# A routed feed-forward behind a linear-attention pipeline: rows ranked and listed by expert sequence by sequence

## The chip, the cores and the metric

The kernel runs on one core of a Trainium2 chip. Time is device time of one launch in microseconds (us), the median of the runs. TensorE is PE in the profile, VectorE is DVE, ScalarE is ACT, GpSimd is POOL, and SyncE, which only issues DMAs here, is SP.

## What is computed

The input x is 8 sequences of 512 rows of 256 floats, 4096 rows in all. First a gated linear attention, then a feed-forward with 8 experts, of which each row uses the one whose centroid it is nearest to:

```python
x = x + attn(layernorm(x), wq, wk, wv, wo, wg1, wg2, norm_w)
z = layernorm(x).reshape(-1, 256)
aff = z @ centroids.T                       # 4096 x 8
assign = argmax(aff, axis=1)
order = argsort(assign)
xs, es = z[order], assign[order]
alpha = sigmoid(aff[order] at es)
for e in range(8):
    h = relu(layernorm(xs, ln_g[e], ln_b[e]) @ w1[e].T + b1[e])
    y = y + where(es == e, xs + h @ w2[e].T + b2[e], 0)
out_sorted = alpha * y + (1 - alpha) * xs
x = x + out_sorted[argsort(order)]
```

The kernel computes each row with its own expert alone. So it must know, for each tile of 128 rows, which expert the tile belongs to and which rows are in it. A tile holds rows of one expert; with 8 experts there are at most 32 + 7 = 39 tiles (`TILES`), and the last tile of an expert is filled up with rows whose result is not written.

## The kernel before

**The pipeline.** `pipeline` runs ten steps (i from 0 to 9) on every engine. In step i, sequence a = i is projected (q, k, v, gate, and GpSimd's tree of decays), sequence b = i - 1 runs the seven levels of the attention scores and its outputs, and sequence c = i - 2 is normed, projected by wo, added to x, normed again (`double_norm`), given its affinities to the centroids (`affinities`, L1215) and written out as rows (`rows_of`, `alphas`, and SP's store to `routed_rows`, L495). The order within a step is written out by hand on each engine in its `step`; engines meet at counting semaphores, and `need(eng, sem, per, s, k)` waits for the k-th count of sequence s. Each engine works strictly in its program's order.

A level of b is a chain: TensorE multiplies (`level`, L885), VectorE updates the operands with decay factors (`update`, L1194) and picks scores under a mask (`pick`, L1205), ScalarE mixes keys (`mix`, L681), and TensorE does the next level. At the end of a step TensorE makes the outputs of b (L976, L977), the affinities of c between them, and VectorE gates the outputs in two halves (`gating`, L1279). The next step begins on TensorE with level 0, half 0, then the transposes of its a (L892), then level 0, half 1.

**The routing.** Behind the pipeline, VectorE takes the affinities of all 4096 rows at once (128 partitions x 32 x 8), finds the expert of each row, and with two matmuls against a triangle of minus ones and a square of ones (L1101, L1102) the rank of each row among its expert's. From it comes a slot (tile and place) of each row; one-hots of tile and place (L1424 to L1432, bf16) and 32 accumulating matmuls (L1107) turn the list round, so that for each slot the row is known. The results are `tile_expert`, `take_idx` (which row to gather) and `put_idx` (where to write it; out of bounds for a filler).

**The tiles.** `rounds` walks the 39 tiles in a hardware loop over groups of four (`SLOTS`), with its first and last turns written out. Per tile: SP loads w1 of the tile's expert (1 MB, L507), GpSimd copies a column of `take_idx` to `take_now` (L644) and gathers 128 rows of 2052 bytes by indirect DMA (L646); TensorE transposes them (L1117), ScalarE applies the expert's gains (L850), TensorE multiplies by w1 (`up`, L1129), VectorE adds b1 (L1459), ScalarE takes the relu (L860), TensorE multiplies by w2 (`down`, L1143), VectorE adds b2 and mixes with the row (L1468, L1473), and GpSimd scatters the 128 results (L654, L657). The gathers run four tiles ahead. SP loads b2 (1 MB, L501) once the last rows are stored; SP, ScalarE, TensorE and GpSimd begin their tiles when `s_idx` stands at 3.

Of the kernel before, what the change touches and what calls it, by code (L numbers as in the profile page):

```python
# [38 lines left out]
ALU = mybir.AluOpType  # L39
ACT = mybir.ActivationFunctionType  # L40
F32 = mybir.dt.float32
# [39 lines left out]
def build_program(nc, x, wq, wk, wv, wo, wg1, wg2, norm_w, centroids_t, ln_g, ln_b, w1_t, b1, w2_t, b2, out):  # L81
# [16 lines left out]
    RW = 2 * D + 1  # L98
    SKIP = 2 * N
# [4 lines left out]

    rows = nc.dram_tensor("routed_rows", (N, RW), F32, kind="Internal").ap()

    ctx = ExitStack()
    with ctx:
# [55 lines left out]
        wo_sb = lay.take(DC * D)  # L164
        row_sb = Layout(ARENA - (TJ * RW + 4), ARENA).take(TJ * RW + 4)[:, 0:TJ * RW]
# [9 lines left out]
        lay2 = Layout(PHASE1_AB, ARENA)  # L175
        WIDE = NT * E
        aff_max = lay2.take(NT)
        is_max = lay2.take(WIDE)
        first = lay2.take(NT)
        onehot = lay2.take(WIDE)  # L180
        count_e = lay2.take(WIDE)
        cum_e = lay2.take(WIDE)
        place = is_max
        slot = lay2.take(NT)
        slot_i = lay2.take(NT).bitcast(I32)
        hi_i = lay2.take(NT).bitcast(I32)
        lo_i = lay2.take(NT).bitcast(I32)
        hi_f = lay2.take(NT)
        lo_f = lay2.take(NT)
        small = lay2.take(12 * E)  # L190
        ntile_i = lay2.take(2 * E).bitcast(I32)
        ge_f = lay2.take(TS * E)
        texp_f = lay2.take(TS)
        slot_f = lay2.take(4 * TS)
        lo_hot = lay2.take(NT * P // 2).bitcast(BF16)
        hi_hot = lay2.take(NT * 3 * TS // 2).bitcast(BF16)
        hot = hi_hot.rearrange("p (t k s) -> p t k s", k=3, s=TS)
        wide = [P, NT, TS]
        iota_r = lay2.take(P)
# [11 lines left out]
        not_below = over_masks[:, 2 * DC * P + D:2 * DC * P + D + P]  # L211
# [5 lines left out]
        aff = sb("aff", [P, NT * E], F32)  # L217
# [6 lines left out]
        put_idx = sb("put_idx", [P, TS], I32)  # L224
        take_now = sb("take_now", [P, SLOTS], I32)
        put_now = sb("put_now", [P, SLOTS], I32)
# [88 lines left out]
        s_r = sem("route_step")  # L315
        s_rank = sem("ranks_done")
        s_hot = sem("onehots_ready")
        s_hot_t = sem("onehots_times_tile_ready")
        s_inv = sem("inverse_done")
        s_idx = sem("indices_ready")  # L320

        s_take = sem("take_idx_ready")
# [9 lines left out]
        s_put = sem("put_idx_ready")  # L332
# [90 lines left out]
        def aff_of(c):  # L423
            if isinstance(c.half, int):
                return aff[:, number(c) * TJ * E:(number(c) + 1) * TJ * E]
            return aff[:, bass.ds(number(c) * (TJ * E), TJ * E)]
# [5 lines left out]

        def ones_wide():
            return ones[:, 0:1].broadcast_to([P, WIDE])

# [30 lines left out]
        def _(sp):  # L466
# [42 lines left out]
            sp.wait_ge(s_idx, 3)  # L509
# [4 lines left out]
        def _(pool):  # L514
            start_at_one(pool, [*s_ve.values(), *s_neg.values(), *s_rstd.values(), *s_shift.values(), s_tree, s_qk, s_q0, s_bscale, s_take, s_put])
# [16 lines left out]
            own(pool.iota(iota_p[:, :], pattern=[[0, 1]], base=0, channel_multiplier=1, allow_small_or_imprecise_dtypes=True))  # L532
            pool.sem_inc(s_const, 1)
# [47 lines left out]

            def step(a, b, c, nxt):
                if c is not None and b is not None:
                    need(pool, s_on, TJ, c, 0)
                    norm("o", c)
                if nxt is not None:
                    need(pool, s_xn, TJ, nxt, 0)
                    norm("x", nxt)
# [23 lines left out]
                if a is not None:  # L612
# [9 lines left out]
            pool.wait_ge(s_aff, NSEQ + 1)  # L622
            made += 1 + 4 * LEVELS
            own(pool.iota(iota_r, pattern=[[1, P]], base=0, channel_multiplier=0, allow_small_or_imprecise_dtypes=True))

            own(pool.memset(not_below, 0.0))
            own(pool.affine_select(out=not_below, in_=not_below, compare_op=ALU.is_gt, fill=-1.0, base=0,
                                   pattern=[[1, P]], channel_multiplier=-1))
            pool.sem_inc(s_const, 1)


            pool.wait_ge(s_hot, 1)
            pool.tensor_tensor(hot[:, :, 2, :], hot[:, :, 0, :], iota_t[:, 0:NT].unsqueeze(2).broadcast_to(wide),
                               ALU.mult).then_inc(s_hot_t, 1)


            pool.wait_ge(s_row_out, 16 * NSEQ + 16)
            pool.wait_ge(s_idx, 3)

            def gather(t):  # L640
                p = t.par

                need(pool, s_yo, 1, before(t, SLOTS), 1)
                pool.tensor_copy(take_now[:, p:p + 1], column(take_idx, t)).then_inc(s_take, 1)  # L644
                need_apart(pool, s_take, 1, t, 1)
                pool.indirect_dma_start(out=gathered[p], out_offset=None, in_=rows,  # L646
                                        in_offset=bass.IndirectOffsetOnAxis(ap=take_now[:, p:p + 1], axis=0)).then_inc(s_rows[p], 16)

            def scatter(t):
                p = t.par  # L650

                if not isinstance(t.half, int) or t.half > 0:
                    pool.wait_ge(s_out[p], t.half * 16)
# [6 lines left out]
            for p in range(SLOTS):  # L660
                gather(Step(0, p, SLOTS))
# [865 lines left out]
```

## Time and profile before

| | us |
|---|---|
| median of 3 runs | 682.22 |
| lowest, highest | 680.75, 683.26 |
| the profiled execution | 684.39 |
| its span | 682.6 |
| PE busy in the span | 597.5 |
| DVE busy | 345.1 |
| ACT busy | 280.0 |
| POOL busy | 225.9 |

The page cuts the span into 40 slices of 17 us. TensorE's busy tenths are 9 from slice 2 to slice 17, then 7, 7, 6, 3, 2 (from about 307 to 392 us), and 9 to the end; its granted clock is 9 in nearly all and falls to 6, 5 there. Every duration is of one execution. "Idle before, releaser" is how long the engine had nothing to run ahead of the row and whose semaphore ended that; "issue" is time in which it waited for nothing that the profile shows. Matmuls are pipelined, and an fp32 matmul shows as more than one row.

### The profile page before, as it was taken

What the parts mean: (1) busy time and instruction counts of PE and PEld (TensorE: products, weight loads), DVE (VectorE), ACT (ScalarE), POOL (GpSimd) and SP (SyncE); (2) the same over time, 40 slices, a digit from 0 to 9 for tenths busy, and PEclk for the clock granted to TensorE, in tenths of its full rate; (3) what the DMA queues carried; (4) which work ended last, traced back from release to release, by engine and by line L of the source; (5) the groups of instructions that cost most, each with busy time, mean ns of one, the idle gap of its engine ahead of it and who ended that gap; (6) DMA issues with size and microseconds to landing.
All of it is one profiled execution on the core that took longest, in us unless ns stands there. A gap on an engine that the chain in (4) does not pass through costs nothing.

```text
span 682.6 us, 12519 instructions
## 1 busy us (share of the span) xinstructions
PE 597.5 (88%) x3638; PEld 503.7 (74%) x3639; DVE 345.1 (51%) x864; ACT 280.0 (41%) x671; POOL 225.9 (33%) x384
## 2 busy tenths in 40 slices
PE   3979998999999899977632499999999999999992
PEld 2547675776868677766521499999999999999992
DVE  2395968859595969677237032233233232332331
ACT  3554766476676667451430122222222222222220
POOL 6614261434434261611012113323323323333321
PEclk9999999999999999979665699999999999999997
DMA  9900015140312302020222855545545546545300
GB/s 318 401 9 1 0 32 94 31 91 15 72 42 70 56 32 63 32 62 32 63 63 72 309 197 209 206 178 190 220 169 209 210 169 218 204 171 222 132 28 2
DMA packets 26844, 83.48 MB, mean 122 GB/s; under 512 B 3437, under 2 KB 13039, under 8 KB 20656
## 3 DMA queue, kind: packets, MB, share of 16 engines
q1 hardware_dynamic: 21120, 67.98, 31.1%
q0 software_dynamic: 4992, 14.45, 5.6%
q10 hardware_dynamic: 688, 0.52, 0.2%
q8 instruction: 21, 0.34, 0.2%
q14 instruction: 23, 0.19, 0.1%
HBM read 70.33 MB, written 13.52 MB: 123 GB/s over the span
## 4 chain that ended last, share of the span: by engine, by line
PE 65%; DVE 10%; DMA 6%; issue 4%; ACT 2%; POOL 1%; DVEq 0%; SPq 0%; POOLq 0%
PE bank_a L1129 21%; PE bank_c L1143 20%; DMA arena<-x 4%; PE bank_l L885 4%; PE bank_c L999 3%; PE bank_a L897 3%; PE bank_a L926 3%; DVE arena L1194 2%; DVE arena L1205 2%; PE bank_a L935 2%; PE bank_b L977 1%; PE bank_b L963 1%; PE bank_b L1117 1%; DMA arena<-routed_rows,take_now 1%; PE bank_a L942 1%
## 5 line engine op out<-in xcount | busy, mean ns | idle before, releaser
L1459 DVE TENSOR_TENSOR arena<-bank_a,b_col 128x512 f32<-128x512 f32 x78 | 54.0, 692 | 193.6 <-PE bank_a L1129 179.8
L1129 PEld LDWEIGHTS bank_a<-masks,arena 128*128 128x128 f32 x1248 | 146.9, 194 | 1.9
L1129 PE MATMUL bank_a<-masks,arena 128*128 128x128 f32 x1248 | 147.0, 277 | 0.0
L1143 PE MATMUL bank_c<-w_sb,arena 128*128 x624 | 141.5, 380 | 1.6 <-ACT arena L860 0.9
L1143 PEld LDWEIGHTS bank_c<-w_sb,arena 128*128 128x128 f32 x624 | 115.5, 190 | 16.8 <-issue 2.7
L885 PEld LDWEIGHTS bank_l<-arena,k_mix 128*128 128x128 f32 x448 | 65.8, 198 | 50.8 <-ACT k_mix L681 37.6
L1194 DVE TENSOR_TENSOR arena<-arena 128x256 f32<-128x256 f32 x224 | 90.4, 445 | 9.6 <-PE bank_l L885 9.4
L860 ACT ACTIVATE arena<-arena 128x512 f32<-128x512 f32 x78 | 45.0, 622 | 107.7 <-PE bank_c L1143 103.3
L885 PE MATMUL bank_l<-arena,k_mix 128*128 128x128 f32 x448 | 73.8, 290 | 16.7 <-DVE arena L1205 14.8
L850 ACT ACTIVATE masks<-bank_b,b_col,g_col 128x128 f32<-128x128 f32 x78 | 31.4, 453 | 132.9 <-PE bank_b L1117 132.9
L897 PE MATMUL bank_a<-arena 128*128 128x512 f32 x160 | 83.5, 621 | 0.0
L681 ACT ACTIVATE k_mix<-arena 128x128 f32<-128x128 f32 x224 | 60.9, 309 | 39.1 <-DVE arena L1194 39.0
L657 POOL DMA_INDIRECT out<-k_mix,put_now x39 | 39.6, 1015 | 51.8 <-issue 39.6
L1205 DVE COPY_PREDICATED arena<-masks,bank_l 128x256 f32<-128x256 uint8 x112 | 51.2, 522 | 0.0
L644 POOL COPY take_now<-take_idx 128x1 int32 (+1 forms) x39 | 7.2, 184 | 132.2 <-DVE k_mix L1473 125.4
L646 POOL DMA_INDIRECT arena<-routed_rows,take_now x39 | 39.0, 999 | 31.0 <-POOL take_now L644 31.0
L598 POOL TENSOR_TENSOR arena<-arena 128x512 f32<-128x512 f32 (+6 forms) x56 | 27.5, 491 | 49.1 <-DVE arena L1238 45.3
L681 ACT ACTIVATE arena<-bank_a 128x512 f32<-128x512 f32 x40 | 23.8, 595 | 46.7 <-PE bank_a L926 29.7
L999 PE MATMUL bank_c<-arena 128*128 128x256 f32 x128 | 35.0, 403 | 3.7 <-ACT arena L681 3.7
L897 PEld LDWEIGHTS bank_a<-arena 128*128 128x128 f32 x160 | 26.8, 200 | 9.7 <-issue 8.9
L1211 DVE TENSOR_TENSOR arena<-bank_a,ident 128x512 f32<-128x512 f32 x16 | 11.0, 687 | 39.5 <-PE bank_a L942 39.5
L926 PE MATMUL bank_a<-arena 128*128 128x256 f32 x128 | 29.1, 380 | 0.9 <-DVE arena L1243 0.9
(137 smaller groups left out, 751.6 us busy)
## 6 DMA issues: line engine op xcount, KB each, us to landing
arena<-w SPq DMA_DIRECT2D x39, 1024.0 KB
routed_rows<-arena SPq DMA_DIRECT2D x8, 1026.0 KB, 8.7
arena<-x SPq DMA_DIRECT2D x16, 512.0 KB, 6.5
w_sb<-w SPq DMA_DIRECT2D x8, 1024.0 KB, 14.7
arena<-b SPq DMA_DIRECT2D x1, 1024.0 KB, 4.6
arena<-routed_rows,take_now POOLq DMA_INDIRECT x39
out<-k_mix,put_now POOLq DMA_INDIRECT x39, 2.5
arena<-wk SPq DMA_DIRECT2D x1, 256.0 KB, 3.9
```

The costliest lines, as they stand in the source:

```text
L657: pool.indirect_dma_start(out=out, out_offset=bass.IndirectOffsetOnAxis(ap=put_now[:, p:p + 1], axis=0), in_=y_out[p], in_offset=None, bou ...
L681: return act.activation(dst, src, ACT.Copy)
L860: act.activation(h_act[:, w], h_sb[:, w], ACT.Relu).then_inc(s_hr, 1)
L885: ins = pe.matmul(bank, k_mix[l % 2][:, m * P:(m + 1) * P], level_queries(buf, m, l), start=True, stop=True)
L897: return pe.matmul(bank[:, :], w[:, i * width + h * P:i * width + (h + 1) * P], xn_t[:, i * T:(i + 1) * T], start=(i == 0), stop=(i == DC ...
L926: m = pe.matmul(bank_a[1 - half][:, j * D:(j + 1) * D], xn_t[:, t0:t0 + P], wv_sb[:, i * D:(i + 1) * D], start=(i == 0), stop=(i == DC - 1))
L999: m = pe.matmul(bank_c[half][:, j * D:(j + 1) * D], o_t[:, t0:t0 + P], wo_sb[:, i * D:(i + 1) * D], start=(i == 0), stop=(i == DC - 1))
L1129: m = pe.matmul(bank_a[k // 4][:, k % 4 * P:(k % 4 + 1) * P], w1_now[t.par][:, i * F + k * P:i * F + (k + 1) * P], xl_t[t.par % 2][:, i * ...
L1143: m = pe.matmul(bank_c[p][:, 0:D], h_act[:, k * P:(k + 1) * P], w2_sb[:, bass.ds(e * (FC * D) + k * D, D)], start=(k == 0), stop=(k == FC ...
L1194: dve.tensor_tensor(half, half, factor(decay[b.par], h, l, second), ALU.mult).then_inc(s_up, 1)
L1205: dve.copy_predicated(picked(attn_t[b.par], l, odd), mask, scores.rearrange("p m (n h) -> p m n h", h=2 ** l)).then_inc(s_pick, 1)
L1459: dve.tensor_tensor(h_sb[:, n * 512:(n + 1) * 512].rearrange("p (k t) -> p k t", t=P), bank_a[n][:, :].rearrange("p (k t) -> p k t", t=P), ...
```

## The change

Three things move or are written anew.

- **Ranking per sequence.** When the affinities of c are there, VectorE runs `route(c)`: the expert of each of the 512 rows, a one-hot laid out by expert, and a running sum along it that carries the number of rows seen so far per expert in its first column. TensorE runs `ranks(c)`: two matmuls of 32 columns that give each row's place in its expert's list. VectorE's `slots` (of the sequence before, in the next step behind level 0) picks the place. GpSimd's `list_rows` writes the row numbers to a table in HBM, `rows_by_expert`, 8 regions of 4096, by four indirect DMAs of 128 numbers of 4 bytes.
- **Tile tables at the end.** What is left behind the pipeline is a matmul of column sums (`s_total`) and small VectorE work on 8 or 40 numbers per partition: for each tile its expert and, per partition, where in `rows_by_expert` its row's number stands (`take_idx`), and `skip` for fillers. The one-hots, the 32 inverting matmuls and GpSimd's product go.
- **GpSimd's turns** are written out, 39 of them without a loop, registers or index copies. The number of each row must now be fetched from `rows_by_expert` (`fetch_ids`, an indirect DMA of 128 numbers, eight tiles ahead at most) before the rows can be gathered; the scatter's index is that number plus `skip`, by a small add on GpSimd. The others begin their tiles when `s_idx` stands at 2, behind `take_idx`.

The diff, cut to its core:

```diff
 # SP, ScalarE, TensorE
-            sp.wait_ge(s_idx, 3)
+            sp.wait_ge(s_idx, 2)
...
 # GpSimd
+            def list_rows(c):
+                n = number(c)
+                need(pool, s_slot, 2, c, 2)
+                pool.tensor_copy(slot_i[:, n * TJ:(n + 1) * TJ], slot_f[:, n * TJ:(n + 1) * TJ]).then_inc(s_sloti, 1)
+                need_apart(pool, s_sloti, 1, c, 1)
+                for j in range(TJ):
+                    t = n * TJ + j
+                    pool.indirect_dma_start(out=listed, out_offset=bass.IndirectOffsetOnAxis(ap=slot_i[:, t:t + 1], axis=0),
+                                            in_=ids[:, t:t + 1], in_offset=None).then_inc(s_listed, 16)
...
                 if c is not None and b is not None:
                     need(pool, s_on, TJ, c, 0)
                     norm("o", c)
+                if c is not None and number(c) > 0:
+                    list_rows(before(c, 1))
                 if nxt is not None:
                     need(pool, s_xn, TJ, nxt, 0)
                     norm("x", nxt)
...
+            list_rows(Step(NSEQ // 2 - 1, 1, 2))
+            pool.wait_ge(s_listed, 16 * NT)
             pool.wait_ge(s_row_out, 16 * NSEQ + 16)
+            pool.wait_ge(s_idx, 2)
...
+            for n in range(SLOTS):
+                fetch_ids(n)
+            for n in range(SLOTS):
+                gather(n)
+                fetch_ids(n + SLOTS)
+            pool.wait_ge(s_idx, 3)
+            for n in range(TILES):
+                if n + SLOTS < TILES:
+                    gather(n + SLOTS)
+                if n + 2 * SLOTS < TILES:
+                    fetch_ids(n + 2 * SLOTS)
+                scatter(n)
...
 # TensorE
+            def ranks(c):
+                need(pe, s_route, 6, c, 6)
+                need(pe, s_x1t, DC, c, DC)
+                pe.matmul(bank_c[1][:, 0:E * TJ], earlier, hot5[:, :, 1:TJ + 1], start=True, stop=False)
+                pe.matmul(bank_c[1][:, 0:E * TJ], ones[:, :], upto5[:, :, 0:TJ], start=False, stop=True).then_inc(s_rank, 1)
...
                 of(b, outputs, 1)
+                of(c, ranks)
...
 # VectorE
                 level(0)
+                if c is not None and number(c) > 0:
+                    slots(before(c, 1))
...
                 output(b, c, a)
+                of(c, route)
...
+            slots(Step(NSEQ // 2 - 1, 1, 2))
+            dve.wait_ge(s_total, 1)
+            own(dve.tensor_copy(end_e, bank_a[0][:, 0:E]))
...
+            dve.tensor_tensor(take_idx[:, :], row, last_row, ALU.min).then_inc(s_idx, 1)
```

`route` is six VectorE instructions of at most 128 x 40 and ends with the running sum; `slots` is two. `gather` and `scatter` wait as before for the tile's `s_yo`, and `gather` also for its ids.

**TensorE at the joint of two steps.** Here TensorE ends the outputs of b (L976 and L977; L983 and L984 in the changed kernel) and begins the next step. Before:

```order
L976 MATMUL bank_b<-arena 128x128
L977 MATMUL bank_b<-arena 128x128
L885 MATMUL bank_l<-arena,k_mix 128x128 [waits level_picked,keys_mixed,q0_ready]
L885 MATMUL bank_l<-arena,k_mix 128x128
L892 MATMUL bank_a<-ident,arena 128x128 [waits attn_diag_set,xn_ready]
L892 MATMUL bank_a<-ident,arena 128x128 x3
```

and now:

```order
L983 MATMUL bank_b<-arena 128x128
L984 MATMUL bank_b<-arena 128x128
L1033 MATMUL bank_c<-arena 128x32 [waits x1t_ready,row_slots_step]
L1034 MATMUL bank_c<-arena,ones 128x32
L892 MATMUL bank_l<-arena,k_mix 128x128 [waits level_picked,keys_mixed,q0_ready]
L892 MATMUL bank_l<-arena,k_mix 128x128
L899 MATMUL bank_a<-ident,arena 128x128 [waits attn_diag_set,xn_ready]
L899 MATMUL bank_a<-ident,arena 128x128 x3
```

The two rank matmuls (L1033, L1034), which wait for `row_slots_step`, the count of `route`, stand ahead of level 0 of the next step.

**VectorE at the same joint.** Behind the second gating (L1279; L1319 now) came the updates of level 0 (L1194; L1201 now) and the sums of the outputs (L1169). Before:

```order
L1211 TENSOR_TENSOR arena<-bank_a,ident 128x512 [waits diag_summed,o_done]
L1279 SCALAR_TENSOR_TENSOR arena<-bank_b,arena 128x512 [waits o_done]
L1194 TENSOR_TENSOR arena<-arena 128x4x64 [waits level_scores]
L1194 TENSOR_TENSOR arena<-arena 128x4x64
L1194 TENSOR_TENSOR arena<-arena 128x4x64 [waits level_scores]
L1194 TENSOR_TENSOR arena<-arena 128x4x64
L1169 BN_STATS o_stat<-arena 128x6 [waits o_gated]
```

and now:

```order
L1319 SCALAR_TENSOR_TENSOR arena<-bank_b,arena 128x512 [waits o_done]
L1242 TENSOR_TENSOR arena<-aff,aff_best 128x32 [waits best_ready]
L1244 SCALAR_TENSOR_TENSOR arena<-arena,iota_e 128x32 [waits row_slots_step]
L1247 TENSOR_REDUCE arena<-arena 128x4 [waits row_slots_step]
L1251 COPY arena<-arena 128x8 [waits row_slots_ready,rows_ranked]
L1253 SCALAR_TENSOR_TENSOR arena<-iota_e,arena 128x4x8 [waits row_slots_step]
L1256 SCALAR_TENSOR_TENSOR arena<-arena 128x40 [waits row_slots_step]
L1201 TENSOR_TENSOR arena<-arena 128x4x64 [waits level_scores]
L1201 TENSOR_TENSOR arena<-arena 128x4x64
L1201 TENSOR_TENSOR arena<-arena 128x4x64 [waits level_scores]
L1201 TENSOR_TENSOR arena<-arena 128x4x64
L1262 TENSOR_TENSOR arena<-bank_c,arena 128x32 [waits rows_ranked]
```

Six instructions of `route` stand between gating and the updates, and the first of `slots` behind the updates.

**GpSimd in a tile turn.** Before, one turn of the loop and its registers:

```order
L644 ISA [waits y_ready]
L644 COPY take_now<-take_idx 128x1
L71 REGISTER_ALU
L646 DMA arena<-routed_rows,take_now 128x513 [waits take_idx_ready]
L654 ISA [waits rows_out1]
L654 COPY put_now<-put_idx 128x1
L657 DMA out<-k_mix,put_now 4096x256 [waits put_idx_ready,y_ready]
```

and now, a turn and the next one's gather:

```order
L653 DMA arena<-routed_rows,id_of 128x513 [waits y_ready,ids_gathered0]
L646 DMA id_of<-rows_by_expert,take_idx 128x1
L658 TENSOR_TENSOR put_of<-id_of,skip 128x1
L661 DMA out<-k_mix,put_of 4096x256 [waits y_ready,put_ready]
L653 DMA arena<-routed_rows,id_of 128x513 [waits y_ready,ids_gathered1]
```

The index copies and registers are gone; a DMA that fetches ids and a small add came in.

## Rows read from the trace of the kernel before

**Rows 1.** The page's head: the span.

```profile
span 682.6 us, 12519 instructions
```

**Rows 2.** Busy us (instructions) of each engine by stretch, then PEclk, DMA share, GB/s.

```profile
20.00:310.00 290.00, 271.63 (x1498) 205.75 (x1497) 216.86 (x600) 181.00 (x471) 107.95 (x162) 0.98 0.24 61
...
350.00:370.00 20.00, 4.64 (x27) 3.25 (x28) 15.83 (x31) 1.14 (x4) 2.69 (x1) 0.50 0.35 105
370.00:390.00 20.00, 7.35 (x46) 6.48 (x45) 3.11 (x10) 2.11 (x5) 4.93 (x8) 0.54 0.70 262
...
420.00:680.00 260.00, 250.15 (x1713) 234.55 (x1711) 79.80 (x140) 66.82 (x136) 81.61 (x137) 0.99 0.47 170
```

**Rows 3.** Chain that ended last, one pipeline step: start us, us, what.

```profile
257.68 0.46 PE bank_l L885 x4
...
278.10 0.87 PE bank_b L950 x6
...
293.79 0.24 PE bank_b L977 x2
294.05 0.69 DVE arena L1279
```

**Rows 4.** Timeline of VectorE at a joint: start us, us, engine, line, what.

```profile
257.72 0.69 DVE L1279 SCALAR_TENSOR_TENSOR arena<-bank_b,arena 128x512 f32<-128x512 f32 x1 [0.60 <-PE bank_b L977]
...
258.33 0.75 DVE L1194 TENSOR_TENSOR arena<-arena 128x256 f32<-128x256 f32 x2
```

**Rows 5.** Timeline: two small VectorE instructions in a row, and TensorE's small matmuls.

```profile
344.47 1.95 PE L1016 MATMUL bank_c<-cent_sb,arena 128*128 128x8 f32 x16 [0.80 <-ACT arena L681]
...
360.63 0.18 DVE L1418 CAST arena<-arena 128x32 int32<-128x32 f32 x1
...
360.84 0.18 DVE L1419 TENSOR_SCALAR arena<-arena 128x32 int32<-128x32 int32 x1
```

**Rows 6.** Waits from 20 to 294 us: us in total, times, longest us.

```profile
DVE x_stat L1169 <- DMA arena<-x: 2.4, 2, 1.6
```

**Rows 7.** Clock: timeline of a TensorE stand and of gatings; windows of 1 us.

```profile
105.18 0.69 DVE L1279 SCALAR_TENSOR_TENSOR arena<-bank_b,arena 128x512 f32<-128x512 f32 x1 [0.60 <-PE bank_b L977]
...
118.96 1.19 PE L885 MATMUL bank_l<-arena,k_mix 128*128 128x128 f32 x4 [2.45 <-DVE arena L1205]
...
145.72 0.69 DVE L1279 SCALAR_TENSOR_TENSOR arena<-bank_b,arena 128x512 f32<-128x512 f32 x1 [0.60 <-PE bank_b L977]
...
182.72 0.69 DVE L1279 SCALAR_TENSOR_TENSOR arena<-bank_b,arena 128x512 f32<-128x512 f32 x1 [0.60 <-PE bank_b L977]
...
119.00:120.00 1.00, 1.00 (x5) 1.00 (x6) 1.00 (x3) 1.00 (x4) 0.92 (x2) 0.50 0.00 0
...
232.00:233.00 1.00, 0.21 (x2) 0.24 (x3) 1.00 (x4) 1.00 (x4) 0.92 (x2) 1.00 0.00 0
```

**Rows 8.** Timeline of GpSimd in a pipeline step, before the x norm.

```profile
231.44 0.28 POOL L557 TENSOR_SCALAR x_neg_mean<-x_mom 128x4 f32<-128x4 f32 x1 [5.80 <-issue]
```

**Rows 9.** Timeline of GpSimd in a tile turn: a gather.

```profile
476.51 0.99 POOL L646 DMA_INDIRECT arena<-routed_rows,take_now  x1 [0.79 <-POOL take_now L644]
```

**Rows 10.** Timeline of the tail, all engines, up to the second tile's transposes.

```profile
346.76 0.19 DVE L1224 TENSOR_REDUCE aff_best<-aff 128x4 f32<-128x32 f32 x1
...
359.15 0.34 SPq L501 DMA_DIRECT2D arena<-b  x1
...
370.39 0.44 DVE L1435 TENSOR_TENSOR arena<-iota_t,arena 128x280 f32<-128x280 f32 x1
...
372.41 0.19 DVE L1447 TENSOR_TENSOR put_idx<-arena 128x40 int32<-128x40 f32 x1
...
376.14 0.99 POOL L646 DMA_INDIRECT arena<-routed_rows,take_now  x1 [0.81 <-POOL take_now L644]
...
384.66 0.69 PE L1117 MATMUL bank_b<-ident,arena 128*128 128x128 f32 x2 [1.40 <-DMA arena<-routed_rows,take_now]
```

**Rows 11.** DMA issues by line: queue, op, count, KB each, us to landing.

```profile
out<-k_mix,put_now POOLq DMA_INDIRECT x39, 2.5
```

More of the change, by code:

```diff
@@ L421, in column, with by_e @@
             return buf[:, bass.ds(number(t), 1)]
[L423 to L426, printed above, removed]
+        def by_e(ap, n=TJ):
+            return ap.rearrange("p (j e) -> p j e", e=E)
+        hot5 = hot.rearrange("p (e j) -> p e j", e=E)
+        upto5 = upto.rearrange("p (e j) -> p e j", e=E)
         def expert_of(t):
@@ L660, in _, with fetch_ids @@
-            for p in range(SLOTS):
-                gather(Step(0, p, SLOTS))
-            def turn(t):
-                if exists(before(t, -SLOTS)):
-                    gather(before(t, -SLOTS))
-                scatter(t)
-            rounds(pool, turn)
+            list_rows(Step(NSEQ // 2 - 1, 1, 2))
+            pool.wait_ge(s_listed, 16 * NT)
+            pool.wait_ge(s_row_out, 16 * NSEQ + 16)
+            pool.wait_ge(s_idx, 2)
+            def fetch_ids(n):
+                pool.indirect_dma_start(out=id_of[:, n:n + 1], out_offset=None, in_=listed,
+                                        in_offset=bass.IndirectOffsetOnAxis(ap=take_idx[:, n:n + 1], axis=0)).then_inc(s_ids[n % SLOTS], 16)
@@ L1347, in step @@
                 output(b, c, a)
+                of(c, route)
                 if b is None:
@@ L1404, in _, with over_tiles, table @@
-            off = small[:, 6 * E:7 * E]
-            own(dve.tensor_copy(upto, cum_e.rearrange("p (e t) -> p e t", e=E)[:, :, NT - 1]))
-            own(dve.tensor_tensor(n_e, upto, prior, ALU.subtract))
+            def over_tiles(ap):
+                return ap.unsqueeze(1).broadcast_to([P, TS, E - 1])
+            def table(ap):
+                return ap[:, 0:TS * (E - 1)].rearrange("p (s e) -> p s e", e=E - 1)
+            slots(Step(NSEQ // 2 - 1, 1, 2))
+            end_e, n_e, nt_e, t_upto, at_e, last_e, d_at, d_last, row_at = (small[:, i * E:(i + 1) * E] for i in range(9))
@@ L1407, in _ @@
+            number_1, picked_e, sum_at, sum_last, row, last_row, beyond = (per_tile[:, i * TS:(i + 1) * TS] for i in range(7))
+            dve.wait_ge(s_total, 1)
+            own(dve.tensor_copy(end_e, bank_a[0][:, 0:E]))
+            own(dve.tensor_tensor(n_e, end_e, region_e, ALU.subtract))
             own(dve.tensor_scalar(ntile_i[:, 0:E], n_e, float(P - 1), None, ALU.add))
@@ L1451, in _ @@
+            own(dve.scalar_tensor_tensor(out=row, in0=beyond, scalar=float(P), in1=row, op0=ALU.mult, op1=ALU.add))
+            own(dve.tensor_tensor(row, row, last_row, ALU.is_gt))
+            dve.tensor_scalar(skip[:, :], row, float(SKIP), None, ALU.mult).then_inc(s_idx, 1)
+            dve.wait_ge(s_idx, 2)
             dve.wait_ge(s_b2, 16)
```

249 lines of the change are left out of this document (108 added, 141 removed).

## The prediction

> **What bounds the kernel now.** The profiled execution has a span of 682.6 us [rows 1] and took 684.39 us in all, so 1.8 us lie around the span; the median of the three runs is 682.22, which is 2.2 us less. I make the sum against 684.39 and take off 2.2 at the end.
>
> I read the busy time by stretch first [rows 2]. It shows three programs behind one another: the attention pipeline (20 to 310 us, TensorE busy 271.63 of 290, VectorE 216.86), the routing between (350 to 390 us, TensorE busy 12 of 40 at half its granted clock), and the expert tiles (420 to 680 us, TensorE 250.15 of 260). The change edits all three, so each is asked for its own bound.
>
> Expert tiles: TensorE alone, 39 tiles in some 290 us from 384.66 to the end, so 7.4 us each. GpSimd's gathers and scatters lie beside it.
>
> Pipeline: the chain of waits over one whole step [rows 3] tells it. From 257.68 the chain is a stretch of TensorE, then VectorE's updates and picks with GpSimd, ScalarE and TensorE answering them, until 278.10; from there to 293.79 it is TensorE without a break; and at 293.79 it hands over from the last output matmul to VectorE's gating at 294.05. No step has slack in this chain, so whatever is put at its joint is paid.
>
> Routing: the timeline from 346.76 to 384.66 [rows 10] is VectorE's long row of rank and one-hot work, then the tile indices, then four gathers, then TensorE's first transposes.
>
> **Part 1, the joint of two steps.** The change puts `route` (six VectorE instructions) behind the second gating, and `ranks` (two matmuls) on TensorE behind the outputs and *ahead of the next step's level 0*. `ranks` waits for `route`, `route` stands behind the gating, and the gating waits for the outputs that TensorE has just finished. TensorE therefore stands still, and with it everything queued behind: level 0 of the next sequence, the transposes of the one after, for whose scores VectorE waits.
> Before, the outputs end at 257.68 and level 0 follows in the same instant [rows 3], while VectorE gates from 257.72 for 0.69 us and starts the first update at 258.33 [rows 4]. Now: gating ends at 258.41. A small dependent VectorE instruction of this size starts 0.21 us behind the one before (360.63 to 360.84) [rows 5]; six are 1.26 us, to 259.67. The two fp32 matmuls show as four rows; sixteen rows of the like took 1.95 us [rows 5], 0.12 each, so 0.5 us, to about 260.2. Level 0 starts 2.5 us late (257.68 to 260.2), and the update that waits for it too. `slots` then puts two more VectorE instructions, 0.42 us, between level 0 and the output sums, again on the chain. Together 2.9 us a joint.
> The joint exists where both a sequence in its last stage and a next step of levels exist: behind steps 2 to 7, six times. 6 x 2.9 = **+17.5 us**. Ends: 2.7 each if the rank matmuls take half of that (16), 3.5 each if each VectorE wait costs 0.3 (21). At the end of step 8 the ranks hide: ScalarE writes the rows of sequence 6 there before it copies what TensorE waits for, and those are eight activations long.
>
> **Part 2, what the delay hides.** VectorE waited 2.4 us in two steps for x to land [rows 6]. Those loads are issued behind the row store, which hangs on the affinities, ahead of the joint; they don't move, VectorE comes 2.9 us later, so the wait goes: **-2.4 us** (ends -2.4 and 0).
>
> **Part 3, the clock.** In the step at 118.96 TensorE had stood for 2.45 us, and the granted clock was 0.50 (1.2 GHz) behind it; near 232, where it was busy for only 0.21 of 1 us in a shorter stand of about 1.6 us, it stayed at 1.00 (2.4 GHz) [rows 7]. That step lasted 40.5 us from gating to gating (105.18 to 145.72) where the next took 37.0; 1.6 of the 3.5 us were its wait for x [rows 6], so 1.9 are the clock's. The new stand is 2.0 us (257.68 to 259.7), between the two. Ends: none of six, all six (11.4). It is halfway between the rows; I take two of six: **+3.8 us**.
>
> **Part 4, listing on GpSimd.** Per sequence a copy and four indirect DMAs, behind the o norm and ahead of the x norm. An indirect DMA keeps GpSimd for 1.0 us, 1.8 with the gap before it [rows 9], so 4.2 to 7.4 us. GpSimd was idle for 5.80 us before the x norm [rows 8]: the x norm may come 2 us late, and ScalarE reads it only behind the last level. Nothing, if that cover holds; gone, with a listing twice as long, the decay tree behind it would be late by some 4 us, and the diagonal matmuls with it. The eleven setup instructions at the start lie in GpSimd's idle time before its first norm: nothing.
>
> **Part 5, the tail.** Kept: the last row store, which lands at 359.15, where SP issues the next load [rows 10]. Removed: the one-hots and the inversion, whose end was the index at 372.41. New: route, ranks and slots end near 349.2 (346.95, then 1.26, 0.5 and 0.42). Behind them GpSimd issues four listing DMAs, to 353.4 or 356.6, landed 2.5 us later [rows 11], by 359. VectorE makes the tables: 25 instructions up to the index, 19 at 0.21 and six of 280 elements at 0.47 (0.44 and its gap [rows 10]), 6.8 us, to 356. So the row store still ends last, at 359.2, and fetching starts 13 us before the old index. But the fetch is a second trip: four id DMAs, then gather 0, one more id DMA and gather 1, the one that `up` of tile 0 stands behind. At 1.8 us an issue gather 1 starts at 370.0, at 1.0 at 365. Its landing: a scatter lands in 2.5 us [rows 11]; the old gather 1, issued at 376.14 beside four 1 MB weight loads, was answered at 384.66, 8.5 us later [rows 10]. The weight loads now start at 359.2 with the bias ahead, 5 MB, over at about 375, so gather 1 sees only their end: I take 5.5, the middle, so 375.5 against 384.66: **-9.2 us**. Ends: 365 + 2.5 (w1 of tile 0 is there by then), -16; 371 + 8.5, -5.
> The Trainium skill (DMA: Bandwidth & Descriptors, Anatomy of one DMA) gives a GpSimd DMA about 2.0 us plus its bytes at 436 GB/s. For a gather of 128 rows of 2052 bytes that is an estimate of 2.6 us, by which the tail would give 12 us and the total be near 689; rows 10 show 8.5 us for the same transfer under load, so the rule does not hold beside the weight loads.
>
> **Part 6, the tile turns.** GpSimd's turn was copy, gather, copy, scatter; now it is gather, id fetch, a small add, scatter, three DMAs at 1.0 to 1.8 [rows 9] and 0.2, so 3.2 to 5.6 us in a TensorE period of 7.4 us. The gathers run four tiles ahead. Nothing; if a fetch took over 3 us, GpSimd would bound.
>
> **Sum:** 684.39 + 17.5 - 2.4 + 3.8 - 9.2 = 694.1; less 2.2 for the median, **691.9 us**, slower by 1.4%.
>
> **Rivals.**
> *The joint is free.* If the level chain had 2.5 us to spare, only the two slots instructions would cost (6 x 0.42 = 2.5) and the tail would decide: 682.2 + 2.5 - 9.2 = 675.5. For it: TensorE idles 18 us in the pipeline stretch. Against: the chain of rows 3 runs through the joint, and in it stands no wait of that size.
> *The tail gives more* and the clock nothing: gathers land in 3 us behind fetches of 1.0 us: -14. 682.2 + 17.5 - 2.4 - 14 = 683.3. For: the small transfers come when much of the weights is in.
> *The clock falls at each joint*: 11.4 - 3.8 = 7.6 on the forecast, 699.5. For: the old stands of 2.45 us.
> *The tail gives nothing* (the change doesn't do what it says): the ids take as long under the weight loads as the gathers did, 8.5 us, and the gathers again; 359.2 + 1 + 8.5 + 3.6 + 8.5 is 381, and with slower issues 385. 691.9 + 9.2 = 701.1. The point is an id landing of over 8 us.
>
> **Chances.** Forecast 0.60; more from the tail 0.15; clock at each joint 0.12; joint free 0.08; tail nothing 0.05. The range leaves out the free joint and the empty tail and a little of the others: 682 to 700. A measurement of this kernel tells about 0.5%, 3.4 us. Faster by more: the free joint and a fifth of the second case, 0.11. Within: half of the second case and the forecast's lower end, 0.13. Slower: 0.76.
>
> **What would show it.** Gating to gating grows from about 37 us by 2 to 3 in each step; TensorE's rank matmul has about 2 us idle before it, released by VectorE's scan, six times; x is no longer waited for; the clock dips behind some joints. From the last row store to TensorE's first `up` about 16 us instead of 26; the last affinity to `up` 29 us instead of 38. The tile period stays. The forecast is wrong if the steps keep their length, if the id fetches land in over 8 us, or if a turn is no longer TensorE's.

## The result and the profile after

The changed kernel takes **720.33 us** (median of 4 runs, 715.55 to 722.29) against 681.49 us for the kernel before (679.94 to 683.26, measured beside it): ratio 1.0572, 95% interval 1.0538 to 1.0607. It is slower, as forecast, but by 39 us where 10 were forecast, outside the range. The profiled execution has a span of 719.4 us.

Busy time by stretch, as in [rows 2]: the pipeline, the two halves of the routing, and the tiles.

```profile
20.00:345.00 325.00, 286.55 (x1535) 217.31 (x1534) 227.39 (x655) 180.45 (x471) 136.02 (x192) 0.95 0.24 54
385.00:405.00 20.00, 0.00 (x0) 0.00 (x0) 6.65 (x28) 4.14 (x9) 4.32 (x5) 0.50 0.64 53
405.00:425.00 20.00, 0.66 (x2) 0.29 (x2) 0.00 (x0) 0.80 (x2) 11.39 (x12) 0.50 0.74 298
455.00:715.00 260.00, 256.20 (x1752) 240.16 (x1750) 82.05 (x144) 67.64 (x138) 103.43 (x137) 1.00 0.49 175
```

The pipeline has grown by 35 us. In the tiles TensorE is a little fuller than before (256 us of 260; 250 before), and a tile still takes 7.25 us in both traces. In the first half of the routing the DMA engines are busy for 0.64 of the time and move 53 GB/s; that is the line to stop at.

The second gating of each step, on VectorE's timeline, answers to the gatings of [rows 7]:

```profile
106.44 0.69 DVE L1319 SCALAR_TENSOR_TENSOR arena<-bank_b,arena 128x512 f32<-128x512 f32 x1 [0.60 <-PE bank_b L984]
148.04 0.69 DVE L1319 SCALAR_TENSOR_TENSOR arena<-bank_b,arena 128x512 f32<-128x512 f32 x1 [0.60 <-PE bank_b L984]
191.43 0.69 DVE L1319 SCALAR_TENSOR_TENSOR arena<-bank_b,arena 128x512 f32<-128x512 f32 x1 [0.60 <-PE bank_b L984]
240.47 0.69 DVE L1319 SCALAR_TENSOR_TENSOR arena<-bank_b,arena 128x512 f32<-128x512 f32 x1 [0.60 <-PE bank_b L984]
```

From one gating to the next the steps last 41.6, 43.4 and 49.0 us, where 37 plus 2.9 was forecast. The joint itself, on the timeline of all engines behind the gating at 191.43, is the forecast one [rows 4]:

```profile
192.04 0.18 DVE L1242 TENSOR_TENSOR arena<-aff,aff_best 128x32 f32<-128x32 f32 x1
...
192.95 0.24 DVE L1256 TENSOR_TENSOR_SCAN arena<-arena 128x40 f32<-128x40 f32 x1
...
193.25 0.41 PE L1033 MATMUL bank_c<-arena 128*128 128x32 f32 x2 [1.86 <-DVE arena L1256]
...
193.72 0.70 PE L892 MATMUL bank_l<-arena,k_mix 128*128 128x128 f32 x4
...
196.47 0.20 DVE L1262 TENSOR_TENSOR arena<-bank_c,arena 128x32 f32<-128x32 f32 x1
```

TensorE idles 1.86 us for `route`, ranks, and takes up level 0 at 193.7, 2.3 us behind the start of the gating. So the rest of the 49.0 us lies elsewhere. The timelines of ScalarE and of TensorE later in the same step:

```profile
215.30 0.60 ACT L738 ACTIVATE arena<-bank_a 128x512 f32<-128x512 f32 x1 [0.87 <-PE bank_a L904]
222.51 0.87 ACT L688 ACTIVATE arena<-bank_b 128x512 f32<-128x512 f32 x2 [6.62 <-remote]
```

```profile
223.26 2.90 PE L970 MATMUL bank_b<-arena 128*128 128x128 f32 x12 [6.15 <-ACT arena L688]
225.95 5.25 PE L933 MATMUL bank_a<-arena 128*128 128x256 f32 x16
```

ScalarE stands for 6.62 us before a copy, released by nothing that the profile can name ("remote" on a kernel of one core), TensorE waits 6.15 us for that copy, and its matmuls behind it run at the lower clock (5.25 us for 16; 3.62 in a mended version). In the waits from 20 to 360 us there are such "remote" rows on ScalarE (10.9 us), VectorE (4.6) and GpSimd (2.4); no such row is in the kernel before, nor in the changed kernel without the listing. The tail, in the chain of waits:

```profile
381.86 0.20 DVE aff_best L1230
...
389.53 0.30 issue
389.84 18.53 DMA rows_by_expert<-arena
408.37 0.26 issue
408.63 5.92 DMA id_of<-rows_by_expert,take_idx
...
417.31 7.96 DMA arena<-routed_rows,id_of
...
425.32 0.69 PE bank_b L1124 x2
```

The last listing DMA is 128 writes of 4 bytes, and it takes 18.53 us. SP's row of waits says that the last row store, issued at 390.06, took as long (before: issued at 351.23, next load at 359.15):

```profile
SPq L495 <- DMA routed_rows<-arena: 17.0, 1, 17.0
```

```profile
388.00:392.00 4.00, 0.00 (x0) 0.00 (x0) 3.57 (x14) 1.96 (x5) 2.43 (x3) 0.50 0.28 96
392.00:396.00 4.00, 0.00 (x0) 0.00 (x0) 0.44 (x3) 0.00 (x0) 0.00 (x0) 0.50 1.48 26
396.00:400.00 4.00, 0.00 (x0) 0.00 (x0) 0.00 (x0) 0.00 (x0) 0.00 (x0) 0.50 1.06 16
```

By windows, the DMA engines are fully busy from 392 to 400 us and move 16 to 26 GB/s. The packets in the trace say who is slow. Those of the listing DMAs (32 bytes, eight entries each) last at most 0.03 us. It is the row store's packets of 2052 bytes behind them that take up to 5.0 us each, where half of them take 0.09; and the packets of the last listing DMA, issued at 389.84, start at 403.1 only, when the row store is nearly through. From the last best affinity to the second tile's transposes it is 43.5 us; before 37.9 [rows 10], forecast 29. One gain was forecast by nobody: from the end of the last scatter to the end of the span it is 8.0 us before and 3.6 in the changed kernel and its variants; with nothing but the turns written out it stays 8.0. Why, these runs don't show.

### The profile page after: what moved, and what is told of

Read it like the earlier page. It is cut to its first block, busy times and chain, and to the rows that moved or that the text cites. A ratio compares the mean times of both kernels' runs of the same rounds, so it can differ in the third digit from the quotient of the medians.

```text
span 719.4 us, 12452 instructions
## 1 busy us (share of the span) xinstructions
PE 608.2 (85%) x3636; PEld 513.6 (71%) x3637; DVE 344.9 (48%) x918; ACT 279.7 (39%) x671; POOL 288.5 (40%) x428
## 4 chain that ended last, share of the span: by engine, by line
PE 72%; DVE 9%; issue 5%; DMA 5%; POOL 3%; ACT 3%; another core or an unknown queue 2%; DVEq 0%; POOLq 0%; ACTq 0%; SPq 0%
PE bank_a L1136 20%; PE bank_c L1150 19%; PE bank_l L892 7%; PE bank_a L904 5%; PE bank_a L933 4%; PE bank_c L1007 4%; DVE arena L1201 3%; DMA rows_by_expert<-arena 3%; PE bank_a L942 2%; PE bank_a L949 2%; DVE arena L1212 2%; PE bank_b L984 2%; PE bank_b L983 1%; PE bank_b L970 1%
## 5 line engine op out<-in xcount | busy, mean ns | idle before, releaser
L1201 DVE TENSOR_TENSOR arena<-arena 128x256 f32<-128x256 f32 x224 | 90.9, 447 | 22.8 <-PE bank_l L892 22.6
L892 PE MATMUL bank_l<-arena,k_mix 128*128 128x128 f32 x448 | 75.8, 296 | 15.7 <-DVE arena L1212 12.2
L653 POOL DMA_INDIRECT arena<-routed_rows,id_of x39 | 37.5, 961 | 127.9 <-DVE k_mix L1486 121.7
L661 POOL DMA_INDIRECT out<-k_mix,put_of x39 | 39.4, 1009 | 45.4 <-POOL put_of L658 28.3
L1124 PE MATMUL bank_b<-ident,arena 128*128 128x128 f32 x78 | 15.5, 281 | 39.9 <-DMA arena<-routed_rows,id_of 39.9
L646 POOL DMA_INDIRECT id_of<-rows_by_expert,take_idx x39 | 36.9, 946 | 29.2 <-DMA rows_by_expert<-arena 17.6
L561 POOL TENSOR_SCALAR o_neg_mean<-o_mom 128x4 f32<-128x4 f32 x8 | 2.3, 291 | 105.5 <-issue 94.2
L594 POOL DMA_INDIRECT rows_by_expert<-arena x32 | 33.7, 1053 | 13.9 <-issue 7.3
L1124 PEld LDWEIGHTS bank_b<-ident,arena 128*128 128x128 f32 x78 | 9.9, 146 | 40.4 <-issue 37.8
```

Of the source, the lines that this page charges most:

```text
L646: pool.indirect_dma_start(out=id_of[:, n:n + 1], out_offset=None, in_=listed, in_offset=bass.IndirectOffsetOnAxis(ap=take_idx[:, n:n + 1], ...
L661: pool.indirect_dma_start(out=out, out_offset=bass.IndirectOffsetOnAxis(ap=put_of[:, n:n + 1], axis=0), in_=y_out[p], in_offset=None, boun ...
L892: ins = pe.matmul(bank, k_mix[l % 2][:, m * P:(m + 1) * P], level_queries(buf, m, l), start=True, stop=True)
L1201: dve.tensor_tensor(half, half, factor(decay[b.par], h, l, second), ALU.mult).then_inc(s_up, 1)
```

## The experiments

Theory T: the listing DMAs hold up the traffic behind them (the clog, below): row stores, loads and whatever ScalarE and VectorE fetch. Rivals: the joint's wait is dearer than it looks (R2); GpSimd's time to issue (R1); the longer GpSimd program (R3). Kernels are the changed one with the edit shown. For each the median is given, and its ratio to the kernel before in the same session, with the 95% interval. A "step" is the time from the second gating of one step to that of the next.

**Leave the listing out.**

```
-                for j in range(TJ): pool.indirect_dma_start(out=listed, ...)
+            for e in range(E): pool.dma_start(listed[region e], ids)      # once, at the start
```

> Left out: the 32 listing DMAs. The table of ids is filled once at the start by eight plain DMAs with ids in another order, so each tile takes rows that are not its expert's; ranks, slots, tile tables, id fetches and gathers all run as in the changed kernel. Theory T (the scattered 4-byte writes hold up the DMA traffic behind them): both the stalls inside the steps and the late row store go. In the changed kernel's profile the pipeline is 34.8 us longer than before, of which about 17.5 to 21 is the wait at the joint, and the fetch of the ids waited 17.6 us at the end. So 690 to 697 us, 24 to 30 us under the changed kernel; the step of sequence 4, 49.0 us there, falls to about 40, and the last row store lands within 8 us. Rival R2 (the joint alone is the cost, the writes are nearly free): at most 8 us saved, 712 or more. Rival R3 (the longer written-out GpSimd code stalls the engines by instruction fetch): no more than 5 us saved, and the waits in the steps stay.

692.65 us (1.0182, interval 1.0151 to 1.0212): 27.7 less than the changed kernel, as T says. This kernel leaves out the lists themselves: its tiles take rows that are not their expert's, in the same number. Its steps are 40.9, 40.8, 39.9, 39.9, 40.9 us; the joint, and the lower clock behind some joints, is all that is left in them.

**Move the ranking off the joint, keep the listing.**

```
 DVE:  level(1); +route(before(c, 1)); level(2); x_stats; +slots(before(c, 1)); level(3)
 PE:   level 2;  +ranks(before(c, 1));  q_proj
 POOL: norm("x", nxt); +list_rows(before(c, 1))      (was ahead of it)
```

> The listing stays, the joint goes: VectorE works out the one-hots of a sequence after level 1 of the next step, TensorE ranks after its level 2, the slots follow before level 3, and GpSimd lists behind the norm of x. Theory T: only the wait of TensorE at the joint goes (1.86 us of idle, 0.63 of ranks and the slots, six times, with what they pushed), 14 to 20 us saved, so 700 to 706 us, and the waits behind the listing DMAs stay wherever they now fall; the step lengths still vary by several us. Rival R2: all of the pipeline's loss was the joint's, 30 us or more saved, 690 or less, with every step at about 37.5 us.

704.4 us (1.0358, 1.0304 to 1.0412), 16 less: T's figure, not R2's. Of the five steps from 106 us on one is 49.2 us, the others 39.0 to 40.2, and ScalarE has a "remote" wait of 4.8 us: the stalls stay and move.

**Entries of 512 bytes.**

```
-                                            in_=ids[:, t:t + 1]
+                                            in_=ids[:, t:t + 128]         # table of 128 words a row
```

> Each entry of the table is 512 bytes wide: a listing DMA still sends 128 descriptors to the same 128 places, but each carries 512 bytes instead of 4, and the id is the first word of it. One small VectorE operation more in the tail (about 0.3 us). Theory T in its form that small writes are what is slow: the stalls in the steps and the 17 us at the end go as without the listing, 691 to 698 us. If it is the scatter and not the size that clogs (rival R4), the time stays at 718 to 725 or rises by what 2.1 MB more cost. Rival R1 (GpSimd's time to issue the DMAs is the cost): unchanged at 719 to 722, since GpSimd does the same work.

689.61 us (1.0128, 1.0089 to 1.0166), 1.4 under T's range. GpSimd issues the same 32 DMAs of 128 descriptors, and 31 us are gone: R1 falls. No "remote" wait is left, and on GpSimd's timeline the first id fetch stands 3.31 us for the list in place of 17.59:

```profile
377.70 0.99 POOL L648 DMA_INDIRECT id_of<-rows_by_expert,take_idx  x1 [3.31 <-DMA rows_by_expert<-arena]
```

**Send each listing DMA twice**, the second into a spare table.

> Each listing DMA is sent twice, the second time into a spare table that nobody reads: 64 instead of 32. Theory T: what the writes cost now, some 25 us, comes once more, 740 to 755 us, with the last row store still later. Rival R2: the writes are nearly free, 720 to 726. Rival R1: GpSimd spends 1.3 us per DMA more, 5.2 us a step, of which it has room for most by the busy shares (GpSimd idles over half of a step), 722 to 735, and the queue's traffic behind them is not later.

740.08 us (1.089, 1.0847 to 1.0933), 20 more: the lower edge of T's range, above R2's and R1's. The "remote" waits grow to 11.5 us at a time (VectorE). The last row store is again waited for 14.3 us and not longer, so the cost grows less than in proportion.

**Both cures at once** (the joint moved, 512-byte entries).

> Both cures at once: 512-byte entries (689.6 us alone) and the ranking moved off the joint (704.4 us alone). If the two costs are separate: the steps of 40.8 us fall to about 37.3, six times 3.5 = 21 us, less what the late ranking still pushes (1 to 4 us): 669 to 673 us, under the kernel before (680). If they overlap (rival: without the clog the joint's wait was hidden in part), 677 to 685.

675.79 us (0.993, 0.9906 to 0.9955): faster than the kernel before by 4, and between my two ranges. The joint's move brought 14 us, not the 21 of separate costs: most steps are 39.0 us. VectorE's timeline has no gap from level 1 to the states there, so 1.0 us of `route` and 0.4 of slots count, and GpSimd's listing, now later, pushes its decay tree into VectorE's level 6 (2.37 us for two updates where 1.35 stood):

```profile
204.48 2.37 DVE L1205 TENSOR_TENSOR arena<-arena 128x256 f32<-128x256 f32 x2
```

**GpSimd's turns written out, alone**, in the kernel before.

```
-            rounds(pool, turn)
+            for n in range(TILES): turn(Step(n // SLOTS, n % SLOTS, SLOTS))
```

> The kernel before with one part of the change alone: GpSimd's 39 expert turns written out in place of a loop. All theories say 0: 679 to 682 us, with a little more instruction traffic at most. Only rival R3 (a longer GpSimd program stalls engines by code loading) expects more than 684.

680.58 us (0.9999, 0.9984 to 1.0014): nothing. R3 falls, the more so as the long program stayed in the kernel without the listing.

**What of the writes is slow: width, or distance?** Entries of 64 bytes; then 4-byte entries spaced out (slot times 128).

> Entries of 64 bytes in place of 4 or 512. If any write under 512 bytes costs the same (a write that has to read first): 715 to 722 us, as the changed kernel. If the cost comes from entries that share one 64-byte line, or falls in proportion with size: near 690 for the first, between 700 and 715 for the second.

> The writes stay 4 bytes wide, but the entries lie 512 bytes apart, as in the table with 512-byte entries. If the size of a write is what costs: 715 to 724 us, as the changed kernel. If it is that neighbouring entries fall into the same piece of memory and wait for each other: 688 to 695.

688.94 us (1.0127, 1.0087 to 1.0167) and 687.0 us (1.0092, 1.0061 to 1.0122). A 4-byte write is not slow by its size: 512 bytes apart, the same writes cost nothing against the kernel without the listing. The Trainium skill (DMA: Bandwidth & Descriptors, Specifications) says that below 512 bytes the engine reads, modifies and writes; these two runs show no price of it here.

**The ranking one step later still**, in VectorE's gap behind the states, with the 4-byte entries 512 bytes apart.

```
 DVE:  states(b); +route(before(c, 1)); output(b, c, a)        next step: level(0); slots(before(c, 2))
 PE:   outputs(b, 1); +ranks(before(c, 1))                     # waits for nothing
```

> Entries of 4 bytes, 512 bytes apart, and the ranking one step later still: VectorE works out the one-hots of a sequence in the next step in its gap behind the states (4.6 us idle before the first diagonal there), TensorE ranks at that step's end without a wait, the slots follow after level 0 of the step behind, GpSimd lists early in that step. What is left of the joint's cost is 0.6 us of ranks and 0.4 of slots per step. If VectorE's fullness between level 1 and the residuals is why the steps of the first mended joint are 39.0 us and not 37.1: steps of 37.5 to 38, six of them 7 us shorter, and 2 for the spaced entries: 666 to 670 us. If not (the listing DMAs or the ranks themselves are the rest): 673 to 677.

671.14 us (0.9869, 0.9846 to 0.9891), 8.8 us under the kernel before, and the best of all, a little above the 666 to 670 that I had put on it. Some 4.5 of the 8.8 us are the shorter end behind the last scatter. TensorE's timeline shows the ranks without a wait between outputs and level 0:

```profile
217.89 0.39 PE L986 MATMUL bank_b<-arena 128*128 128x128 f32 x2
218.11 0.31 PE L1036 MATMUL bank_c<-arena 128*128 128x32 f32 x2
218.25 0.39 PE L1037 MATMUL bank_c<-arena,ones 128*128 128x32 f32 x2
218.48 0.70 PE L894 MATMUL bank_l<-arena,k_mix 128*128 128x128 f32 x4
```

and the chain of waits its tail, 27.8 us from the best affinity to the second transposes:

```profile
346.50 0.20 DVE aff_best L1236
...
354.51 3.88 DMA rows_by_expert<-arena
...
359.94 6.21 DMA id_of<-rows_by_expert,take_idx
...
366.41 7.83 DMA arena<-routed_rows,id_of
...
374.28 0.69 PE bank_b L1130 x2
```

**How far apart?** 16 bytes; 64 bytes with the first moved joint; 8 bytes.

> Entries of 4 bytes, 16 bytes apart: four to a piece of 64 bytes in place of sixteen. If writes into the same small piece wait for each other, with 64 bytes the piece: between the dense table (720) and the spaced one (687), about 692 to 705. If the piece is 16 bytes or less: 685 to 690. If it is larger than 64, up to 512 bytes (the 64-byte entries' 688.9 speaks against it): above 705.

> Entries of 4 bytes, 64 bytes apart, and the ranking moved off the joint as in the first mended version. If 64 bytes between the entries are enough: 672 to 676 us, as with 512-byte entries (675.8) or 1 to 3 us less. If they are not enough: over 680.

> Entries of 4 bytes, 8 bytes apart. At 4 bytes apart the kernel takes 720, at 16 bytes 689.6, at 512 bytes 687.0. If the cost falls with how many entries share a small piece of memory, and faster than their number: 692 to 705. If only entries that touch each other wait (some merging or ordering of adjoining writes): 687 to 691. If anything nearer than 16 bytes is as bad as adjoining: 712 or more.

689.55 (1.0136, 1.0103 to 1.0168), 674.48 (0.9916, 0.989 to 0.9941) and 690.1 us (1.0164, 1.0102 to 1.0225). Even 8 bytes are enough, so my picture of entries that share a 64-byte piece fell. But each spaced table was also larger, and its regions further apart: 32 KB with 8 bytes, 64 KB with 16, 2 MB with 512, always a power of two.

**Taken apart.** `REGION = 2 * N`; adjoining entries of 8 bytes; 4-byte entries at odd words; and the table moved by an unused tensor of 128 KB.

> Dense 4-byte entries as in the changed kernel, but the experts' regions lie 32 KB apart instead of 16 KB (the table is twice as large). If adjoining 4-byte entries are the cause: 716 to 724. If it is the distance between the experts' regions, which every spaced table changed too, or the size of the table: 686 to 692.

> Entries of 8 bytes, adjoining, the id in the first word. If writes that adjoin each other are slow whatever their width: 712 or more. If it is two writes into one 8-byte word: 687 to 692, since here each entry has an 8-byte word of its own.

> Entries of 4 bytes, 8 bytes apart, at the odd words of the table. If a write that starts off an 8-byte boundary is what is slow (half the dense entries do, none of the spaced tables' did): 712 or more. If it is two entries in one 8-byte word, or adjoining ones: 687 to 692.

> The changed kernel with an unused DRAM tensor of 128 KB declared ahead of the table, so that the table lies elsewhere. If the place of the table in memory decides: anything down to 687. If it does not: 716 to 724.

699.75 (1.025, 1.0186 to 1.0313), 688.92 (1.0111, 1.0073 to 1.0149), 691.33 (1.0147, 1.0115 to 1.0179) and 709.84 us (1.0442, 1.0406 to 1.0478). Adjoining writes and odd words are not slow in themselves. Dense entries still cost some 10 us with the regions 32 KB apart, which neither of my readings had (716 to 724, and 686 to 692). And in another place the same table costs 20 us in place of 30: the place counts, 10 us of it, but is not all.

**The two left, each alone.** Dense entries, regions 17,472 bytes apart (`REGION = N + 272`); and entries 8 bytes apart in a table of the dense one's 128 KB, with regions of 16,384 bytes (`REGION = N // 2`).

> Dense 4-byte entries; the experts' regions 17,472 bytes apart in place of 16,384, so that no power of two lies between them. If the regions' distance is what collides: 686 to 692. If density decides and distance only helps a little: 698 to 722.

> Entries of 4 bytes, 8 bytes apart, but each expert's region holds 2048 entries in place of 4096 (enough for these inputs): the table has the 128 KB, the place and the 16 KB between regions of the dense one. If the space between entries is what cured the spaced tables: 687 to 692. If it was the size or the regions' distance that came with it: 700 to 724.

689.91 (1.0158, 1.0114 to 1.0203) and 694.62 us (1.0203, 1.0143 to 1.0263). With dense 4-byte entries one number, 4096 to 4368, takes 30 us away. Spacing the entries alone, in the dense table's size, place and regions, brings nearly as much (5 us less), which is between my two ranges again. So neither the density nor the regions' distance does it alone: all the spaced tables had regions a power of two apart, and the dense one with shifted regions was as dense as ever. The full 30 us take both. My reading is that the eight experts' regions fill at about the same pace, so that the places being written lie nearly the regions' distance apart, all 32 DMAs long, and collide when that is a power of two and the entries are dense. It rests on one distance that is no power of two; that 17,472 bytes are good for another reason, the place of the regions say, which alone is worth 10 us, was not tested. The gatings with the regions shifted, on VectorE's timeline:

```profile
188.53 0.69 DVE L1319 SCALAR_TENSOR_TENSOR arena<-bank_b,arena 128x512 f32<-128x512 f32 x1 [0.60 <-PE bank_b L984]
229.36 0.69 DVE L1319 SCALAR_TENSOR_TENSOR arena<-bank_b,arena 128x512 f32<-128x512 f32 x1 [0.60 <-PE bank_b L984]
269.25 0.69 DVE L1319 SCALAR_TENSOR_TENSOR arena<-bank_b,arena 128x512 f32<-128x512 f32 x1 [0.60 <-PE bank_b L984]
```

The packets in the traces tell it within each kernel, whatever the session. Of the 9728 packets of x loads and row stores (1024 and 2052 bytes) between 60 and 400 us, so many take over 2 us, in one execution of each:

| kernel | packets over 2 us | longest, us |
|---|---|---|
| before | 4 | 3.5 |
| without the listing | 0 | 1.8 |
| changed: dense, regions 16 KB apart | 103 | 5.5 |
| the same, table moved | 60 | 4.3 |
| dense, regions 32 KB apart | 19 | 3.6 |
| every 8 bytes, regions 16 KB apart | 22 | 3.6 |
| every 8 bytes, regions 32 KB apart | 1 | 2.2 |
| dense, regions 17,472 bytes apart | 1 | 2.2 |
| entries of 512 bytes | 0 | 1.9 |

And the writes outlive their own packets. In the step of 191.43 the last of them is sent at 207.0, and from 208 to 218.2 the trace has a single DMA packet, one of instructions; yet the x load that begins at 218.3 has packets of up to 4.1 us. So what they wait for is no other packet that the trace has. That it is the memory's channels or banks which collide is inferred; no run here looks inside. The Trainium skill (DMA: Bandwidth & Descriptors, Latency and other measured facts) tells of tiles whose rows lie 512 KB or more apart at powers of two, up to half the rate lost, and advises padding. Here it is scattered single words at 16 KB, and the one padding tried, of 1 KB, was enough. The changed kernel itself was not run again in the session of these two, so their distance to 720 spans sessions, and chips, on which the tables may lie elsewhere (the kernel before gave 680.07 there, 681.49 then); the sessions with 704 and 740 us beside 689.6, and with 710 beside 689 to 691, hold dense and mended tables side by side.

## Why the prediction was wrong

**Part 1, the joint: right.** Six waits of TensorE for VectorE's scan, 11.1 us, and a gap to level 0 of 2.3 us (forecast 2.5), plus 0.4 for the slots. Steps without the clog and without a clock fall last 39.9 us against 37.0 [rows 7]: 2.9, the forecast figure.

**Part 2, x: the wait is gone, its reason not shown.** The wait for x [rows 6] is gone in the four mended versions whose waits I read (without the listing, 512-byte, spaced, shifted regions). But the kernel before with GpSimd's turns written out, which has no delay at its joints, shows none either, and its steps there are 37.0 us, the one of 40.5 [rows 7] too. So the 2.4 us may be a matter of the profiled execution, and not of the joint.

**Part 3, the clock: the term was mis-sized both ways.** With the regions shifted it fell behind three of the first five joints (the sixth has a fall before the change too). Two windows:

```profile
192.00:196.00 4.00, 4.00 (x15) 2.80 (x14) 2.52 (x12) 2.08 (x6) 0.23 (x2) 0.57 0.80 214
233.00:237.00 4.00, 4.00 (x21) 2.44 (x18) 3.40 (x15) 2.82 (x9) 0.84 (x3) 1.00 0.68 195
```

The granted clock is 0.57 behind the joint at 188.53, whose step takes 40.8 us, and 1.00 behind that at 229.36, whose step takes 39.9: 0.9 us a fall, where I had taken 1.9, from the same single step. Three falls are 2.7 us for the 3.8 of the sum. From the second gating of its first step to that of its last, that kernel takes 270.5 us; the kernel before took 256.5 in its profiled execution, and 250.3 in that with GpSimd's turns written out: 14 to 20 us more, where Parts 1 to 3 came to 18.9.

**Part 4, "Listing on GpSimd ... Nothing, if that cover holds": this step failed.** As to GpSimd it is true: the norm of x came late, and it was waited for 0.9 us once, as before. But I asked only what the DMAs cost the engine that *issues* them, and looked for their price in the nearest row, a scatter of 128 whole rows that lands in 2.5 us [rows 11]. Their cost fell on everybody else's transfers: about 19 us in the pipeline (first gating to last: 289.8 us against 270.5 with the regions shifted) and 12 in the tail.

**Part 5, the tail: its own mechanism right, its listing wrong.** "Four listing DMAs ... landed 2.5 us later" was 18.53 us, and "the row store still ends last, at 359.2" was a row store of 17 us, both through the same clog. Freed from it, the tail gives what was forecast (29 us from the best affinity to the second transposes, before 37.9): 27.8 with spaced entries and the late ranking, 31.5 with the regions shifted, where the last row store took 8.4 us. Inside, two errors cancelled: gather 1 took 7.8 us, not 5.5, but was issued 19.9 us behind the best affinity, not 23.2 (GpSimd's issues are 1.27 us apart, not 1.8). That they cancelled is luck. And the end of -16 should read -17: 365 + 2.5 against 384.66.

**Part 6 and the rivals.** The tile turns cost nothing, as said; the tile period is 7.25 us before and after (not the 7.4 of the prediction). None of the four rivals was it: two of them asked how long gathers and fetches of ids take to land, none what the listing's own writes might do. The missing one, "the listing lands late and holds up others", was in reach: Part 5 bounded the landing of gather 1 by two rows 6 us apart, and gave the listing's landing a single value.

## What to carry to other kernels

Give a DMA that the trace has never shown two prices, what it costs its issuer and what it costs the traffic behind it, and bound both; a busy DMA share at few GB/s, and "remote" waits on a single core, are what the second looks like. Where several lists of small entries grow side by side in DRAM, dense and a power of two apart, try another distance or entries with space between them; here either was worth 25 to 30 us. And ranking work belongs in an engine's own gap a step later, not between the last matmul of a step and the first of the next.

## What the runs showed of the hardware

- 4096 indirect writes of 4 bytes, densely into eight DRAM regions 16,384 bytes apart, cost the kernel 30 us more than into regions 17,472 bytes apart (689.9 us) or as 512-byte entries (689.6). Densely 32,768 bytes apart they cost 10 us more, and 16,384 apart with entries at every 8 bytes 5.
- Their packets last 0.03 us at most. What is slow are other packets, up to 5.5 us each, and still so 11 us after the last of the writes was sent.
- While they clog, the row store's descriptors of 2052 bytes go at 16 to 26 GB/s, and the list DMA's completion takes 18.53 us against 3.88.
- ScalarE stood for 6.6 us and VectorE, with the listing sent twice, for 11.5 with no releaser in the profile during such a clog. I suspected that they wait for their instructions, which are packets in the same trace. While ScalarE stands (215.9 to 222.5 us) no such packet is recorded, so the trace doesn't bear that out; the cause is open.
- GpSimd issues indirect DMAs 1.27 us apart (1.0 busy, 0.30 between); 0.8 us lie ahead of the first one behind a copy.
